# A graph network's two layers on one core: every fifth group of tiles counted during the messages, the messages' sum as one product and a fold

## The reference, cut to what matters

```
h = relu(layernorm(x))
edge = mlp(attr4)                                  # 4 -> 96: relu, then mean and variance over all edges
msg  = mlp([h[src], h[dst], edge])                 # 288 -> 96: relu, then mean and variance over all edges
x = x + segment_sum(msg, dst) + mlp(h)
h = relu(layernorm(x))
f = segment_sum((h @ W_gcn)[src] * dinv[src] * dinv[dst], dst)     # dinv = 1/sqrt(degree)
x = x + relu(f @ W1 + b1) @ W2 + b2
```

## Time and profile before

| what | value |
|---|---|
| runs, median of 3 | 6530.68 us (6529.23 to 6531.93) |
| the profiled execution's own time | 6520.64 us |
| its span, first to last instruction | 6518.9 us |
| busy: PE, DVE, ACT, POOL | 5654.6, 4173.9, 3822.2, 3237.0 us |
| messages, stretch | 919 to 4341 us |
| counting, stretch | 4627 to 6452 us |

### The profile page before, as it was taken

How to read it: one execution, slowest core, us unless ns; L and a number is a source line. 1 busy time by engine, 2 the same in 40 slices (tenths; PEclk the granted TensorE clock), 3 DMA queues, 4 the chain that set the end, 5 groups by cost and what they waited for, 6 DMA issues and landing times. The chain is left out here.

```text
span 6518.9 us, 128731 instructions
## 1 busy us (share of the span) xinstructions
PE 5654.6 (87%) x38038; PEld 4382.9 (67%) x38038; DVE 4173.9 (64%) x13072; ACT 3822.2 (59%) x7170; POOL 3237.0 (50%) x3406
## 2 busy tenths in 40 slices
PE   6755559999999999999999999977799999999998
PEld 5311127777777777777777777765477777777777
DVE  5577764545454544445454444553799999999996
ACT  3566644434444444444444444433699999999996
POOL 3577757777777777777777777753000000000000
PEclk8555555555555555555555555555799999999998
DMA  4444433333333333333333333321000000000001
GB/s 155 137 123 124 124 83 74 74 76 75 76 75 76 74 76 74 74 76 75 75 75 76 74 75 75 74 79 30 18 2 2 2 2 2 2 2 2 2 2 62
DMA packets 297570, 400.07 MB, mean 61 GB/s; under 512 B 146679, under 2 KB 203015, under 8 KB 296247
## 3 DMA queue, kind: packets, MB, share of 16 engines
q1 hardware_dynamic: 193543, 233.00, 12.1%
q0 software_dynamic: 103344, 158.83, 11.5%
HBM read 333.74 MB, written 57.67 MB: 60 GB/s over the span
## 5 line engine op out<-in xcount | busy, mean ns | idle before, releaser
L932 POOL DMA_INDIRECT gbuf<-a_tab,idxb x2688 | 2580.4, 960 | 859.0 <-issue 812.3
L1718 ACT ACTIVATE nf<-psum 128x600 bf16<-128x600 f32 x3234 | 1824.2, 819 | 4.8 <-PE psum L1709 4.8
L1017 PEld LDWEIGHTS psum<-rhs,lhs 128*128 128x128 f32 x6448 | 1434.3, 327 | 365.8 <-issue 365.8
L1017 PE MATMUL psum<-rhs,lhs 128*128 128x96 f32 x6448 | 1628.7, 434 | 13.5 <-DVE rhs L975 13.5
L1038 ACT ACTIVATE msg<-pre 128x384 f32<-128x384 f32 x806 | 421.8, 523 | 1991.2 <-DVE pre L1030 1988.7
L1030 DVE TENSOR_TENSOR pre<-psum,gbuf 128x384 f32<-128x384 f32 x806 | 448.2, 556 | 1613.6 <-issue 1130.0
L1709 PE MATMUL psum<-x_all 128*128 128x300 bf16 x6468 | 1358.8, 291 | 121.6 <-DVE x_all L1702 44.6
L1061 PE MATMUL psum<-oh,msg 128*97 128x32 f32 x6448 | 1171.1, 344 | 282.4 <-ACT msg L1038 276.7
L1061 PEld LDWEIGHTS psum<-oh,msg 128*97 128x97 f32 x6448 | 1134.0, 282 | 364.1 <-ACT msg L1038 358.7
L1701 DVE TENSOR_SCALAR x_all<-x_all,dstrel 128x600 bf16<-128x600 f16 x3234 | 1193.8, 369 | 87.4 <-PE psum L1709 63.0
L1731 PE MATMUL psum<-x_all,nf 128*128 128x96 bf16 x15400 | 1074.4, 205 | 1.0 <-ACT nf L1718 1.0
(11 more groups left out here) (198 smaller groups left out, 3340.3 us busy)
## 6 DMA issues: line engine op xcount, KB each, us to landing
gbuf<-a_tab,idxb POOLq DMA_INDIRECT x3224
x_all<-dst_row SPq DMA_DIRECT2D x403, 128.0 KB
x_all<-attr_parts SPq DMA_DIRECT2D x807, 36.0 KB
x_all<-attr_parts SPq DMA_DIRECT2D x1209, 24.0 KB
spilled<-gbuf SPq DMA_DIRECT2D x134, 192.0 KB, 1.9
gbuf<-spilled SPq DMA_DIRECT2D x134, 192.0 KB
x_all<-b_tab SPq DMA_DIRECT2D x806, 12.0 KB
attr_parts<-sT SPq DMA_DIRECT2D x72, 136.0 KB, 1.9
```

Of the source, the lines that this page charges most:

```text
L932: g.indirect_dma_start(gbuf[:, k % 4, t, :], None, a_tab[:, :], bass.IndirectOffsetOnAxis(ap=idxb[:, k % 4, t:t + 1], axis=0)).then_inc(g_ ...
L1017: ins = pe.matmul(ps_m(k)[:, t, :], lhs[:, k % 2, t * TILE:(t + 1) * TILE], rhs[:, k % 2, :], start=True, stop=True)
L1718: act.activation(adj[:, g % 2, :, j * SLOT:(j + 1) * SLOT].rearrange("p (b h) s -> p b h s", b=2), ps_a(n).rearrange("p b (h s) -> p b h s ...
```

## The change

One group of tiles in five (groups 4, 9, ..., 149: 30 groups, 630 tiles) is counted during the messages. In steps 0 to 20 of every 26, one early tile is handled: VectorE makes its two one-hots, TensorE makes the two halves of its counts one after the other in the single bank 7, with the message product between them, and ScalarE copies each half into `stage`. After 21 tiles ScalarE's queue stores `stage` (two transfers, 3.2 MB together) to `adj_tab` in device memory. Keys are worked out group by group by six small chained operations.

In the counting stage 124 late groups remain. An early group's counts are read back by four transfers into four "homes" in free memory, and its 100 products are spread over the 42 tiles of two windows in four; late groups' products now lie in the last 14 tiles of a window.

The sum of the messages of a step is one f32 product, all 128 one-hot columns against all 4 x 97 message columns. Its four diagonal blocks are what is wanted: ScalarE copies them from PSUM (`keep_blocks`) and a product with four stacked 32 x 32 identities adds them up (`fold_blocks`). The pipeline is longer by three steps: `add_window` handles step k-5. The attributes are loaded by one transfer in place of three, the destinations for one step at a time.

```diff
+EARLY = 26
...
+        self.early = [g for g in range(4, self.NG, 5)][:self.SV // EARLY]
+        self.late = [g for g in range(self.NG) if g not in self.early]
+        self.NE, self.ND = len(self.early), len(self.late)
...
-            for j in range(PARTS):
-                r = j * PARTS * KE
-                sp.dma_start(rk[r:r + PARTS * KE, b, :, :].rearrange("p s e -> p (s e)"),
-                             attr_rows[:, bass.ds(e0, HP * ES)]).then_inc(r_land[b], 16)
-            sp.wait_ge(ohT_ok.sem, ohT_ok.at(MT * i + k + 1 - 4))
+            sp.dma_start(rk[:, b, :, :].rearrange("p s e -> p (s e)"),
+                         attr_rows[:, e0:e0 + HP * ES].unsqueeze(0).to_broadcast([PARTS, PARTS * KE, HP * ES])
+                         ).then_inc(r_land[b], 16)
...
+        def load_targets(sp, i, k):
+            if msgs.absent(i, k):
+                return
+            sp.wait_ge(ohT_ok.sem, ohT_ok.at(MT * i + k - 2))
             sp.sem_inc(turn, 1)
-            sp.dma_start(dstbc[C:P, b, :, :].rearrange("p s e -> p (s e)"),
-                         a["dst_row"][:, bass.ds(e0, HP * ES)].partition_broadcast(W)).then_inc(d_land[b], 16)
+            sp.dma_start(dstbc[C:P, k % 2, :],
+                         a["dst_row"][:, bass.ds((MT * i + k) * ES, ES)].partition_broadcast(W)).then_inc(d_land[k % 2], 16)
...
-            pe.wait_ge(s_add.sem, s_add.at(MT * i + k - 2))
+            pe.wait_ge(d_ok.sem, d_ok.at(MT * i + k - 2))
+            pe.matmul(ps_s(k), oh[:, k % 4, :, :].rearrange("p t w -> p (t w)"),
+                      msg[:, k % 2, :, :].rearrange("p t c -> p (t c)"), start=True, stop=True).then_inc(s_mm.sem, 1)
+        def keep_blocks(act, i, k):
+            if msgs.absent(i, k):
+                return
+            act.wait_ge(s_mm.sem, s_mm.at(MT * i + k))
+            act.wait_ge(f_mm.sem, f_mm.at(MT * i + k - 2))
             for t in range(SUP):
-                ins = pe.matmul(ps_s(k), msg[:, k % 2, t, :], oh[:, k % 4, t, :], start=(t == 0), stop=(t == SUP - 1))
-            ins.then_inc(s_mm.sem, 1)
+                ins = act.activation(diag[t * W:(t + 1) * W, k % 2, :],
+                                     ps_s(k)[t * W:(t + 1) * W, t * (C + 1):(t + 1) * (C + 1)], ACT.Copy)
+            ins.then_inc(d_ok.sem, 1)
+        def fold_blocks(pe, i, k):
+            if msgs.absent(i, k):
+                return
+            pe.wait_ge(d_ok.sem, d_ok.at(MT * i + k))
+            pe.wait_ge(s_add.sem, s_add.at(MT * i + k - 1))
+            pe.matmul(ps_f(k), diag[:, k % 2, :], sel, start=True, stop=True).then_inc(f_mm.sem, 1)
         def add_window(dve, i, k):
             if msgs.absent(i, k):
                 return
             base = dve.value_load(base_i[:, bass.ds(MT * i + k, 1)], min_val=0, max_val=N - 1)
-            dve.wait_ge(s_mm.sem, s_mm.at(MT * i + k))
+            dve.wait_ge(f_mm.sem, f_mm.at(MT * i + k))
             dve.wait_ge(s_add.sem, s_add.at(MT * i + k - 1))
             cols = sT[0:C + 1, bass.ds(base, W)]
-            dve.tensor_tensor(cols, cols, ps_s(k), ALU.add).then_inc(s_add.sem, 1)
+            dve.tensor_tensor(cols, cols, ps_f(k), ALU.add).then_inc(s_add.sem, 1)
...
+        def early_tile(k):
+            g, j = k // EARLY, k % EARLY
+            return (g, j, g * GT + j) if g < NE and j < GT else None
+        def early_keys(dve, k):
...
+            link(dve.tensor_scalar(hi_e, src, 9, 2, ALU.logical_shift_right, ALU.logical_shift_left))
+            link(dve.tensor_scalar(two_e, src, 3, None, ALU.bitwise_and))
+            link(dve.tensor_tensor(hif_e, hi_e, two_e, ALU.add))
+            link(dve.scalar_tensor_tensor(keys[:, e % 2, :], hif_e, float(SLOT), rel_e[:, e, :], ALU.mult, ALU.add))
+            link(dve.tensor_scalar(two_e, src, 2, P - 1, ALU.logical_shift_right, ALU.bitwise_and))
+            link(dve.tensor_copy(lows[:, e % 2, :], two_e))
+        def early_onehots(dve, k):
+            tile = early_tile(k)
+            if tile is None:
+                return
+            e, j, n = tile
+            if n >= 2:
+                dve.wait_ge(n_mm, 2 * (n - 1))
+            dve.tensor_scalar(key_e[:, n % 2, :], iota_ke, keys[:, e % 2, j:j + 1], None, ALU.is_equal)
+            dve.tensor_scalar(low_e[:, n % 2, :], iota_le, lows[:, e % 2, j:j + 1], None, ALU.is_equal).then_inc(n_oh, 1)
+        def early_counts(pe, k, b):
+            tile = early_tile(k)
+            if tile is None:
+                return
+            n = tile[2]
+            if b == 0:
+                pe.wait_ge(n_oh, n + 1)
+            if n or b:
+                pe.wait_ge(n_ok, 2 * n + b)
+            pe.matmul(bank[7][:, 0:HB], low_e[:, n % 2, :], key_e[:, n % 2, b * HB:(b + 1) * HB],
+                      start=True, stop=True).then_inc(n_mm, 1)
+        def early_keep(act, k, b):
+            tile = early_tile(k)
+            if tile is None:
+                return
+            e, j, n = tile
+            act.wait_ge(n_mm, 2 * n + b + 1)
+            if j == 0 and b == 0 and e:
+                act.wait_ge(o_adj, 32 * e)
+            act.activation(stage[:, b * HI // 2:(b + 1) * HI // 2, j * SLOT:(j + 1) * SLOT],
+                           bank[7][:, 0:HB].rearrange("p (h s) -> p h s", s=SLOT), ACT.Copy).then_inc(n_ok, 1)
+        def early_store(act, k):
+            tile = early_tile(k)
+            if tile is None or tile[1] != GT - 1:
+                return
+            e = tile[0]
+            act.wait_ge(n_ok, 2 * GT * (e + 1))
+            for b in range(2):
+                act.dma_start(adj_tab[e, :, b * HI // 2 * QS:(b + 1) * HI // 2 * QS],
+                              stage[:, b * HI // 2:(b + 1) * HI // 2, :].rearrange("p h s -> p (h s)")).then_inc(o_adj, 16)
...
-                    for x in (r_mm, m_mm, s_mm):
+                    for x in (r_mm, m_mm, s_mm, f_mm):
                         x.start(pe)
...
                     def step(i, k):
                         edge_product(pe, i, k)
+                        early_counts(pe, MT * i + k, 0)
                         message_product(pe, *msgs.earlier(i, k, 1))
+                        early_counts(pe, MT * i + k, 1)
                         sum_edges(pe, *msgs.earlier(i, k, 2))
-                    msgs.run(pe, step, 2)
+                        fold_blocks(pe, *msgs.earlier(i, k, 4))
+                    msgs.run(pe, step, 4)
                 @block.scalar
                 def _(act):
-                    for x in (r_ok, m_ok, m_sq):
+                    for x in (r_ok, m_ok, m_sq, d_ok):
                         x.start(act)
                     def step(i, k):
                         copy_indices(act, i, k)
                         edge_relu(act, *msgs.earlier(i, k, 2))
+                        early_keep(act, MT * i + k - 2, 0)
+                        early_keep(act, MT * i + k - 2, 1)
+                        early_store(act, MT * i + k - 2)
                         message_relu(act, *msgs.earlier(i, k, 3))
                         square(act, *msgs.earlier(i, k, 3))
-                    msgs.run(act, step, 3)
+                        keep_blocks(act, *msgs.earlier(i, k, 4))
+                    msgs.run(act, step, 4)
+                    act.wait_ge(o_adj, 32 * NE)
                 @block.vector
                 def _(dve):
                     dve.memset(sT[:, 0:NP], 0.0).then_inc(m0, 1)
                     dve.memset(acc[:, :, :], 0.0).then_inc(m0, 1)
+                    dve.tensor_reduce(sel, ident[:, :].rearrange("p (t w) -> p w t", w=W), AX, ALU.add).then_inc(sel_ok, 1)
                     dve.wait_ge(m0, 2)
+                    dve.wait_ge(n_iota, 1)
+                    dve.tensor_copy(iota_ke, iota_e).then_inc(n_rel, 1)
+                    dve.wait_ge(n_rel, 1)
+                    dve.tensor_copy(iota_le, iota_p[:, :])
+                    dve.wait_ge(n_first, 1)
...
                     for x in (ohT_ok, w_ok, m_pre, m_acc, s_add):
                         x.start(dve)
                     def step(i, k):
                         onehot_T(dve, i, k)
                         window_rows(dve, i, k)
+                        early_keys(dve, MT * i + k)
+                        early_onehots(dve, MT * i + k)
                         onehot(dve, i, k)
                         add_gathered(dve, *msgs.earlier(i, k, 1))
                         accumulate(dve, *msgs.earlier(i, k, 2))
-                        add_window(dve, *msgs.earlier(i, k, 2))
-                    msgs.run(dve, step, 2)
+                        add_window(dve, *msgs.earlier(i, k, 5))
+                    msgs.run(dve, step, 5)
...
+        homes = [(50, x_flat[:, 0:50 * QS // 2 + 1]),
+                 (24, gbuf[:, :, :, :].rearrange("p k t c -> p (k t c)")[:, 0:24 * QS // 2 + 1]),
+                 (16, lhs[:, :, :].rearrange("p b e -> p (b e)")[:, 0:16 * QS // 2 + 1]),
+                 (10, sq[:, :, :, :].rearrange("p k t c -> p (k t c)")[:, 0:10 * QS // 2 + 1])]
...
+        def early_load(sp, e):
```

(109 more changed lines are left out.)

132 lines of the change are left out of this document (92 added, 40 removed).

## The result

The changed kernel takes 6334.59 us (median of 4 runs, 6324.51 to 6350.95); before it was 6530.79. The ratio is 0.9702, 95% interval 0.968 to 0.9724: 3% faster. I had forecast 6660, slower, with a range of 6450 to 6800, so the prediction was wrong in its sign and its range.

A forecast was written before the change was run, and what follows sets the result against it. Gathers were taken to pace the messages, ScalarE's copies the counting. 6520.6 + 455 (messages) - 337 (counting) + 15 (setup, tail) = 6654; the median lies 10 above, 6664, rounded to 6660; range 6450 to 6800.

The forecast's parts named there:

- What bounded the kernel before: Gathers pace the messages at 4.21 us a step, TensorE close behind at 3.74; ScalarE's copies, 0.564 each, fill the counting.
- The circle: Messages, early steps: add, early one-hots, count product, message product, next add wait on each other, 4.68 to 4.96 us.
- its signs: Messages: add waits for TensorE, GpSimd for the add hundreds of us, count products for the low one-hot; clock 0.50.
- I take 4.9, since TensorE's clock stayed at 0.50 through the messages: Messages: an early step priced at 4.9 us at half clock, so the stage takes 3846 against 3391, 455 more.
- Clock up: Rival, messages: more streaming raises TensorE's granted clock, early steps fall to 4.68 us, total 6541 or 6523; chance 0.15.
- At full clock the message product gains nothing: Messages: a 128-column-weight f32 product of 96 columns starts every 0.47 us at either clock, so an early step falls only to 4.68.
- TensorE's own work: Messages: one f32 product 1.30 us, fold 0.34; TensorE needs 4.54 to 4.86 us an early step, 4.04 in others.
- Keys, setup: Messages: six chained key operations every 26 steps, 1.15 us; setup and the longer tail, 15 us in all.
- Stores: Rival, messages: the 3.2 MB store holds ScalarE's queue 8 us or lands late, 150 to 240 us more; chance 0.13.
- The one-hots and GpSimd: Messages: new one-hots lengthen GpSimd's gathers by 0.05 us a step, 45 us at most; with an exclusive lock up to 0.6 a step.
- that rival: Messages: early one-hots are ready before TensorE needs them, steps stay at the gathers' pace, total 6255; chance 0.10.
- The counting: Counting stretch: 630 fewer tiles save 355 us, early sums crowding 60 windows cost 18 (12 to 54); 337 given back.

The follow-up runs named there:

- the sum alone: The changed kernel without early groups; the one f32 product, the copies of its blocks and the fold stay: 6530.15 us, ratio 1.001.
- the early counts with the old sum: The changed kernel with the four f32 sum products again, without block copies and fold, `add_window` at step k-2: 6907.8 us, ratio 1.0589.
- The strided run: The changed kernel with the message product taking every fourth column as weights, in place of neighbouring ones: 6775.82 us, ratio 1.0387.
- the fastest: The changed kernel with early tiles counted a step later, stores spread over five steps, early sums in a window's first seven tiles: 6221.97 us, ratio 0.9543.

## Why the prediction was wrong, point by point

*What bounded the kernel before* was right: with the sum alone, TensorE became quicker and the time stayed.

*The circle* was right in place and, at half clock, in size: 4.77 and 4.87 us measured for 4.68 to 4.96. Of its signs one failed even so: GpSimd waits for ScalarE's index copies and hardly for the add. The step "I take 4.9, since TensorE's clock stayed at 0.50 through the messages" failed. I carried a clock over from a kernel whose products the change replaces. The sum alone shows that the replacement raises it, 0.50 to 0.71; the early counts with the old sum show that they alone don't. The replacement is the one product together with its fold and the longer lag. No run takes these apart, so which of them the clock answers to stays open. The five steps of 26 without early tiles, which I had put at 4.1 us, took 4.35 at half clock (2516.09 to 2520.44 from add to add).

*The rival "Clock up"* named this and was mispriced by the step "At full clock the message product gains nothing". It took the price from the node stage's products, whose weights are read with a step of four; the message product's are neighbours. At full clock it takes 1.10 us, not 2.02. With 1.14 for 2.06 the circle's low end of 4.68 would have been 3.76 (3.88 measured), below the gathers' 4.21, and the messages would have been forecast within a few us of before plus what stores and half-clock stretches cost. The strided run confirms this from the other side: with the node stage's pattern the whole kernel takes 6776, slower than before and 116 above my 6660, though its clock still alternates (0.50 and 1.00 in the windows above).

On the clock I had cited the Trainium skill (TensorE: Matmul & The Clock Gate, "The HAM clock gate") and held the kernel before against it. The runs leave it there: with the sum alone TensorE is busy 2592 of 3200 us at 0.71, before it was 3121 of 3422 at 0.50. The busier engine had the lower clock, though part of that is effect and not cause: at half clock the same message product lasts 1.98 us in place of 1.10.

*TensorE's own work.* One product over 388 columns took 1.30 us at half clock (2427.59 to 2428.89 in the changed kernel, start to start), as scaled from the 512-column row, and 0.85 busy at full clock. The fold's 0.34 was 0.40 and 0.26.

*Keys, setup.* One group's six key operations took 1.29 us (2522.28 to 2523.57) for 1.15. What lies around the two stretches grew by 8.1 us for 15.

*Stores.* The rival saw ScalarE's queue held for 8 us; it was 0.81. The price came by gathers that the stores held up, 55 to 64 us in all, within the 0 to 100 I gave, by a mechanism that I hadn't named.

*The one-hots and GpSimd.* I gave them at most 45 us (that rival's sum makes 6254, not 6255); the gathers' mean rose by 6 ns in the changed kernel and by 12 in the fastest, which would be 16 and 32 us. The exclusive lock of the Trainium skill (SBUF — State Buffer, "SBUF: two separate sides") would have given up to 0.6 us a step if these one-hots are such two-port operations; whether they are, no run here shows, and no delay of that size appears.

*The counting* was mis-sized in one term. I took 18 us for the 60 crowded windows, within 12 to 54; 1528.7 is 60 above 2604 tiles at 0.564, and putting the early sums where the others are absent gave back 47.

## What to carry to other kernels

Price an operation from a row with the same access pattern, not only the same shape and type: here a step of four in the weights hid a factor of two. When a change replaces TensorE's products, treat its clock as part of the result, work the chain out at both levels, and see on which side of the present bound each falls. A large store issued at once can stop an engine that never touches it, by way of the small gathers it needs; spread it over the steps.

## What the runs showed of the hardware that I had not expected

An f32 weight load of 128 neighbouring columns took 0.12 us a record at full clock (0.97 for eight), at half clock 0.22 (1.78 for eight). Read with a step of four it took 0.24 at either (1.94 for eight). Two stores of 1575 KB drove the transfer engines to 400 GB/s, and for 4 of these 8 us the gathers' queue moved nothing, in the other 4 us 0.19 MB, though GpSimd's issuing went on at 1.25 us each.
